# Turning the near value rows by fp32 products over all 128 rows instead of 32-row transposes

## The reference, cut to what matters

```python
# B, L = 2, 1024; 8 heads; latent rows c_kv have 32 values, rope rows 32 values
I = where(local, inf, I); I = where(causal, -inf, I)      # local: the last 64 keys of a query
_, idx = top_k(I, 96)                                     # 64 local keys and 32 selected ones
key_c = (c_kv @ W_uk)[bi, idx];  value = (c_kv @ W_uv)[bi, idx]
key_r = _pope((x @ W_kr)[bi, idx], angles_k)              # rotated by its place in the list
scores = (q_c . key_c + q_r . key_r) * scale              # per query, head and selected key
out = softmax(scores) @ value                             # per query and head
```

## Time and profile before

| | |
|---|---|
| time, median of 3 runs | 1869.62 us (1869.48 to 1874.66) |
| span of the profiled execution | 1877.9 us, 8.3 us above that median |
| instructions | 32172 |
| TensorE matmuls | 1499.3 us busy, 80% of the span, 10722 instructions |
| TensorE weight loads | 954.4 us, 51%, 10788 |
| VectorE | 1244.6 us, 66%, 2571 |
| ScalarE | 1058.8 us, 56%, 1832 |
| GpSimd | 451.3 us, 24%, 751 |
| chain that ended last, by engine | TensorE 52%, VectorE 12%, ScalarE 10%, "issue" 10%, "another core or an unknown queue" 5% |

### The profile page before, as it was taken

The page is one execution under the profiler, slowest core; times in us unless marked ns, Lnnn a source line. Parts: engine busy times, 40 slices in busy tenths (PEclk is TensorE's granted clock), DMA queues, the critical chain, the costliest instruction groups (busy, mean ns, idle before and its releaser), DMA issues.

```text
span 1877.9 us, 32172 instructions
## 1 busy us (share of the span) xinstructions
PE 1499.3 (80%) x10722; PEld 954.4 (51%) x10788; DVE 1244.6 (66%) x2571; ACT 1058.8 (56%) x1832; POOL 451.3 (24%) x751
## 2 busy tenths in 40 slices
PE   3899997799957464878777888777589999689995
PEld 2455554577743112544554555555345555457774
DVE  3777774677784566666566676634377777457777
ACT  2477775688836333434444444333247777558883
POOL 4122222000010501343434343440422222200000
PEclk8799998799977557988878888778679999869998
DMA  5211100112111243111111111120321110011110
GB/s 156 72 41 40 41 28 1 58 68 72 52 47 52 67 99 80 48 33 48 53 45 56 30 56 49 33 70 11 111 69 42 40 41 28 1 58 68 67 56 23
DMA packets 61959, 98.92 MB, mean 53 GB/s; under 512 B 19819, under 2 KB 41779, under 8 KB 59766
## 3 DMA queue, kind: packets, MB, share of 16 engines
q1 hardware_dynamic: 52182, 79.64, 13.6%
q0 software_dynamic: 8192, 16.79, 3.4%
q10 hardware_dynamic: 1456, 0.84, 0.2%
HBM read 73.42 MB, written 10.69 MB: 45 GB/s over the span
## 4 chain that ended last, share of the span: by engine, by line
PE 52%; DVE 12%; ACT 10%; issue 10%; another core or an unknown queue 5%; DVEq 4%; DMA 2%; SPq 1%; ACTq 1%; POOL 0%; POOLq 0%
PE twin L953 9%; PE twin L943 6%; PE twin L802 6%; PE twin L747 4%; PE twin L781 4%; ACT arena L1174 4%; PE twin L1107 4%; DVEq L1736 3%; ACT experts L1247 2%; PE twin L752 2%; PE twin L1135 1%; PE twin L1123 1%; PE twin L1151 1%; PE twin L812 1%
## 5 line engine op out<-in xcount | busy, mean ns | idle before, releaser
L1174 ACT ACTIVATE arena<-twin 128x1024 f32<-128x1024 f32 x288 | 294.7, 1025 | 122.3 <-PE twin L781 119.0
L725 POOL DMA_INDIRECT arena<-kv_rows,IDX x256 | 248.6, 971 | 451.6 <-PE twin L1154 313.4
L1427 DVE TENSOR_REDUCE arena<-twin 128x8 f32<-128x1024 f32 (+1 forms) x160 | 195.4, 1225 | 75.0 <-PE twin L752 37.6
L1476 DVE TENSOR_TENSOR experts<-arena,experts 128x512 fp32r<-128x512 f32 x256 | 171.6, 690 | 71.2 <-ACT experts L1247 71.2
L1245 ACT ACTIVATE arena<-twin,bias 128x512 f32<-128x512 f32 x256 | 185.5, 725 | 45.9 <-PE twin L943 45.8
L943 PE MATMUL twin<-experts,experts 128*128 128x512 f32 x768 | 196.8, 403 | 7.4 <-ACT experts L1247 5.4
L1418 DVE TENSOR_REDUCE arena<-twin 128x2 f32<-128x1024 f32 x128 | 153.4, 1223 | 63.6 <-PE twin L747 61.1
L747 PE MATMUL twin<-ffn,ffn 64*128 64x128 f32 (+3 forms) x1152 | 151.9, 346 | 49.5 <-DMA arena<-arena 26.5
L1247 ACT ACTIVATE experts<-twin,bias 128x512 fp32r<-128x512 f32 x256 | 186.9, 730 | 0.0
L1800 DVE TENSOR_TENSOR HN<-twin,RT 96x512 f32<-96x512 f32 x128 | 87.4, 683 | 148.9 <-remote 86.0
L953 PE MATMUL twin<-experts,experts 128*128 128x512 f32 x768 | 182.2, 389 | 0.0
(11 more groups left out here) (251 smaller groups left out, 2367.4 us busy)
## 6 DMA issues: line engine op xcount, KB each, us to landing
arena<-wt_rows SPq DMA_DIRECT2D x16, 1024.0 KB, 4.8
arena<-in_L_ffn_w SPq DMA_DIRECT2D x32, 256.0 KB, 5.2
ffn<-q_rows SPq DMA_DIRECT2D x64, 128.0 KB
ffn<-k_rows SPq DMA_DIRECT2D x64, 128.0 KB
XT<-idx_rows SPq DMA_DIRECT2D x16, 512.0 KB
q_rows<-ffn SPq DMA_DIRECT2D x8, 512.0 KB, 4.8
k_rows<-ffn SPq DMA_DIRECT2D x4, 1024.0 KB, 9.2
arena<-kv_rows,IDX POOLq DMA_INDIRECT x256
```

The source lines that it names most:

```text
L725: pool.indirect_dma_start(G[d % GR][:, g, :], None, kv_rows, bass.IndirectOffsetOnAxis(ap=IDX[:, q, k * GB + g:k * GB + g + 1], axis=0))\
L1174: act.activation(PT[(UNITS * buf + u) % PT_RING].rearrange("p s n -> p (s n)"), twin[2 * u % S_RING][:, :], ACT.Exp, scale=float(HD) ** -0 ...
L1427: dve.tensor_reduce(to, scores.rearrange("p (s t k) -> p s t k", s=2, t=to.shape[2]), AX_X, ALU.max).then_inc(max_done, 1)
L1476: dve.tensor_tensor(H1R[tb % 2][1][:, f, :], H1[tb % 2][:, f, :], H1R[tb % 2][0][:, f, :].bitcast(F32), ALU.subtract)\
```

## The change

The four transposes of a near block, each with 32 partitions of `GTS` as weights and a 32x32 piece of the identity as moving operand, become four products: each has all 128 partitions of `GTS` as weights and the identity's columns 64 to 95 as moving operand. Column j of that operand picks partition 64 + j, so the output is the same 128 x 32 tile. Nothing else differs.

```diff
@@ -1135,8 +1135,8 @@ def pe_turned(pe, x):
                 m = pe.transpose(bank[6][:, part * P:(part + 1) * P], PB[x % 3][:, part * P:(part + 1) * P], ident)
             if not far:
                 for g in range(GB):
-                    m = pe.transpose(bank[6][:, 2 * P + g * DC:2 * P + (g + 1) * DC],
-                                     GTS[x % 3][2 * DR:ROWKV, g * P:(g + 1) * P], ident[2 * DR:ROWKV, 2 * DR:ROWKV])
+                    m = pe.matmul(bank[6][:, 2 * P + g * DC:2 * P + (g + 1) * DC], GTS[x % 3][:, g * P:(g + 1) * P],
+                                  ident[:, 2 * DR:ROWKV], start=True, stop=True, skip_group_check=True)
             m.then_inc(tp_done, 1)
```

## The result

The changed kernel takes 1898.8 us (median of 4, 1898.3 to 1902.9) against 1869.6 us for the kernel before (1869.4 to 1874.7). The ratio is 1.012, 95% interval 1.009 to 1.0151: slower, by some 22 us by the ratio and 29 us by the medians. The ratio of the medians themselves, 1.0156, lies just outside that interval, so the size is known only as somewhere between 20 and 30 us. The forecast was +8.

The account below looks back on a forecast made before the run. TensorE updates released late beside gathers bound the early loop, TensorE alone the tail. 2.3 us (last six blocks) + 4.7 (half of 18 blocks) + 1 (newly on the chain) = +8 on 1869.6: 1877.6 us, range 1874 to 1884, over all cases 1862 to 1896.

Parts of the forecast that it names:

- The price of the pieces: TensorE turning of a near block at full clock: 0.52 us removed, 0.90 us added, net +0.38 us.
- The sum over the loop: Added TensorE work over 64 near blocks, full and half clock mixed at 0.52 us each: 33 us.
- The factor of four: Transposes four times faster for fp32: products 1.48 us, +0.96 us a near block, 61 us in all; not used.
- what of it lies on the path: Share of the loop's 33 us of added TensorE work that lengthens the run: +8 us, the rest hidden by late updates.
- half of the 18: 18 near blocks on the chain amid gathers, half of them counted as exposed: 9 x 0.52 = 4.7 us.
- one mean of 0.52 us: Net added turning per near block over the loop, 0.7 at full clock (+0.38) and 0.3 at half (+0.85).
- Rival A: Switching into and out of 32-row shape beside gathers holds TensorE's updates; removing it gives 1800 us; chance 0.08.
- The argument that line 1154's update was due before the first transpose: In one loop episode that update was due 0.3 us before the 32-row transposes, yet came late too.
- that of the setup: Setup, 619 to 653 us: 24 gathers beside products, one wait of 0.6 us, so a gather alone is not enough.
- Rival B: Gathers alone set the updates' release; all added turning hidden except 2.3 us in the last six blocks: 1872; chance 0.30.
- Rival C: Turned tiles reach ScalarE late in every near block, all added work exposed: +33 us, 1903; chance 0.10.
- Rival D: Fuller TensorE lifts the loop's granted clock from 0.85 to 0.88, saving 15 us: 1863; chance 0.09.

Follow-up runs that it names:

- e4: Changed kernel with its four full-row products per near block issued twice; 1985.4 us, ratio 1.0605 against the kernel before.
- e3: Changed kernel with the fp32 products taken over the 32 latent rows alone, so the old tile shape stays; 1908.9 us, ratio 1.0159 against the kernel before.
- e2: Kernel before with the four 32-row transposes of each near block issued twice; 1886.1 us, ratio 1.0072.
- e1: Kernel before with near rows not turned at all from the fifth block on (output wrong); 1877.2 us, ratio 1.0015.
- e9: Changed kernel run again in a later job without new edit, beside the kernel before; 1771.6 us, ratio 1.0091.
- e7: Kernel before with the near turning moved ahead of TensorE's wait for the softmax; 1744.1 us, ratio 0.9933.

## Why the prediction was right in direction and too small

*The price of the pieces* held. Removed 0.37 + 0.15 us: measured 0.37 and, by the 0.47 left of line 1101, 0.12. Added 0.90 us: measured 0.81 for the first eight, and 1.71 for sixteen in e4, so 0.90 for the eight further ones, which is line 894's step of 0.112 us. Net +0.32 for +0.38 us. At half clock I had 1.71 us; it is 1.55. What I called the change of tile shape, 0.15 us behind the transposes, is only one end of it: the other end lay inside the 0.37 us (the late weight loads above), which leaves the sum as it was. The Trainium skill, "TensorE: Matmul & The Clock Gate", section "LDWEIGHTS (loading the stationary operand)", says that a weight load takes its columns over 1.2 GHz, whatever the rows; for 128 columns that is an estimate of 107 ns. The products agree with it, 0.10 to 0.11 us each over 128 rows, and over 32 rows 0.125 with the change of shape in it (e3). The old transposes, with 128 columns too, do not: four more in e2 took 0.24 us, 0.06 us each.

*The sum over the loop* held: 33 us of TensorE work forecast, 36.6 us of busy time measured. Part of that is luck: 14 of the 64 near blocks before and 16 to 18 after had their turning at half clock, about a quarter and not 30%. The factor of four that the prediction took from the Trainium skill, "TensorE: Matmul & The Clock Gate", section "Terms", was set aside for the wrong reason. Four further transposes cost 0.24 us (e2) and the products that do the same 0.90 us (e4), 3.7 times as much, so these traces come near the factor. The 61 us did not come because the prediction multiplied the 0.37 us, with the change of shape in it.

*The step that failed* is what of it lies on the path. "The chain passes through the old transposes in only 24 of 64 near blocks" and "I count half of the 18" gave 8 us of 33. Measured is 20 us in the loop of the two traces and 22 us by the ratio. (The trace has 23 pieces, so 17 amid gathers; counting all of them in full would still have given only 2.3 + 8.8 + 1 = 12 us.) I took the present chain as the measure of what an addition would do. It is no such measure, and not one of a removal either: e1 took the turning out for nothing, while e2 added 15 us at full clock and cost 14. The chain now crosses the turning in 29 blocks and spends 22 us more there (31.6 against 9.3), and it spends less on late updates and more on "issue". So more of the blocks were near the path than lay on it, and the late updates covered less than I had assumed. How many blocks have how much slack, no run shows.

The clock is a second term that I mis-sized. I priced exposed and hidden blocks with one mean of 0.52 us, but 11 of the 29 crossings now are at half clock, 17 of the 31.6 us, while only 5 to 7 of the 35 near blocks off the chain are. Before the change there was no such tilt: 5 of 23 crossings and 9 of the other 41. So the tilt is seen in one trace of the changed kernel, and no run isolates it.

*Rival A* fell in e1: 209 us of "remote" waits with no 32-row transpose left, against 246. The argument that line 1154's update was due before the first transpose was sound; that of the setup was weak, since TensorE ran 13 matmuls in those 34 us and stood idle until 637.7, and e9 is what shows that gathers alone are not enough. The drain that the Trainium skill, "TensorEngine Tiling (Array Packing)", section "Key Properties", tells of costs 0.12 us here behind the turning (0.59 against 0.47) and about 0.2 us ahead of it, not 2 to 3.5. *Rival B* (+2.3) is outside the interval. *Rival C* (+33, 1903) is outside as well, above 1.0151 x 1869.6 = 1897.8, though the medians' +29 comes close to it; the truth lies between it and the forecast. *Rival D* asked for a granted clock of 0.88 and it stayed 0.85.

*The signs named beforehand:* 512 and 512 instructions, yes. A piece near 0.9 us in the tail, 0.81. Line 1101 at 0.44 behind it, 0.47. The remote waits "still near 110 and 86": 85.8 and 88.0, with 27 us more on line 1809, the sum the same. The gap between ScalarE's copies in the tail "longer by about 0.4 us": up to the two near blocks it went from 2.56 and 2.70 us to 3.00 and 3.04, and a round of four blocks from 10.14 to 10.82 us, 0.34 us a near block.

*What stays open:* what holds TensorE's updates in the held condition. Shown is that it needs no 32-row instruction (e1), and that the same gathers run without it in the free condition (e9). In the traces of the held condition it comes only in the part of the loop that has gathers, but no held run without gathers was obtained. Open too is whether leaving out the turning would gain something in the free condition, where e7's move did.

## What to carry to other kernels

An fp32 product in place of a transpose cost twice the weight loads and twice the products here, and 0.90 us where four transposes of this shape cost 0.24. Widening from 32 to 128 rows cost nothing and saved the change of tile shape, 0.3 us a block, so the two should be judged apart. The share of the chain that a line has now does not tell what more work there costs: measure a doubling as well as a removal, for the two can answer differently. And work that does not depend on the awaited result belongs ahead of the wait; here that gained 0.6 to 0.7% in the free condition.

## What the runs showed that I had not expected

The same kernel takes 1875 us in one job and 1756 us in others, the job's other kernels moving with it, and the difference is in one stretch: the loop takes 587 us in the first trace of the changed kernel and 458 us in e9, its "remote" waits going from 247 us to under 10. TensorE's granted clock rises with it from 0.85 to 0.96. The cost of the change is about 1% in both (1.012 and 1.0091), and e7's gain is known for one of them alone.
